# A four-layer block on one core: another order of the instruction lists of three engines in layer 1

## The reference, cut to what matters

```python
xn = _layernorm(x)                      # x already holds layer 0, its experts' output included
# attention: 16 heads of 64, causal
q, k, v = (einsum('bsd,hda->bhsa', xn, W) + b for W, b in ((Wq, bq), (Wk, bk), (Wv, bv)))
pattern = softmax(where(causal, q @ k.T * scale, -100000.0))
x_attn = einsum('bsha,had->bsd', pattern @ v, Wo) + bo
# feed-forward: both operands rounded to FP4 in blocks of 16 along the last axis
def fp4_quant_dequant(x):               # blocks of 16: scale = max|x| / 6
    idx = searchsorted([0.25, 0.75, 1.25, 1.75, 2.5, 3.5, 5.0], abs(x / scale))
    return GRID[idx] * sign(x) * scale
h = silu(fp4(xn) @ fp4(w_gate).T) * (fp4(xn) @ fp4(w_up).T)      # 352 wide
x = x + x_attn + fp4(h) @ fp4(w_down).T
```

## Time and profile before

| what | us |
|---|---|
| median of three executions | 3218.11 (3212.95 to 3218.94) |
| the profiled execution, whole | 3212.44 |
| its span from first to last instruction | 3211.1 |
| busy in the span: PE | 2501.2 |
| busy in the span: DVE | 2231.2 |
| busy in the span: ACT | 1427.3 |
| busy in the span: POOL | 835.2 |
| granted clock of TensorE, mean | 0.904 |

### The profile page before, as it was taken

The page is one execution under the profiler, slowest core; times in us unless marked ns, Lnnn a source line. Parts: engine busy times, 40 slices in busy tenths (PEclk is TensorE's granted clock), DMA queues, the critical chain, the costliest instruction groups (busy, mean ns, idle before and its releaser), DMA issues.

```text
span 3211.1 us, 47743 instructions
## 1 busy us (share of the span) xinstructions
PE 2501.2 (78%) x18201; PEld 1749.2 (54%) x18201; DVE 2231.2 (69%) x4587; ACT 1427.3 (44%) x3688; POOL 835.2 (26%) x453
## 2 busy tenths in 40 slices
PE   4788888888887767888888888867999975677776
PEld 2455555556555654555656556544666663454444
DVE  3488888888887544666576666644666626999997
ACT  0344534544445114565555656532433333444443
POOL 0033343333444301222222222210000002333332
PEclk9899999999999877999999999977999997888887
DMA  1010110110111440000000000000000003444342
GB/s 58 21 34 28 47 35 28 41 41 28 41 41 40 136 168 1 1 1 1 1 1 1 1 1 1 1 32 13 27 27 14 8 25 109 147 128 153 127 152 86
DMA packets 71348, 147.97 MB, mean 46 GB/s; under 512 B 6864, under 2 KB 37072, under 8 KB 70608
## 3 DMA queue, kind: packets, MB, share of 16 engines
q1 hardware_dynamic: 69072, 140.73, 13.3%
q0 software_dynamic: 2048, 4.20, 0.4%
HBM read 135.20 MB, written 9.18 MB: 45 GB/s over the span
## 4 chain that ended last, share of the span: by engine, by line
PE 29%; DVE 16%; issue 13%; ACT 9%; POOL 5%; DMA 2%; SPq 0%; DVEq 0%; POOLq 0%; ACTq 0%
POOL h L2054 4%; ACT pr L1764 3%; PE psum L578 2%; DVE mx L1282 2%; PE psum L325 2%; PE psum L470 2%; PE psum L504 2%; PE psum L515 2%; PE psum L582 2%; PE psum L347 2%; DVE mx L1326 1%; PE psum L774 1%; ACT pt L1808 1%; PE psum L587 1%; POOL got L2045 1%
## 5 line engine op out<-in xcount | busy, mean ns | idle before, releaser
L2020 POOL TENSOR_TENSOR h<-h,Crep 128x1024 f32<-128x1024 f32 x128 | 383.5, 3006 | 700.9 <-DVE h L1444 700.9
L2002 POOL TENSOR_TENSOR pr<-pr,rsum 128x512 f32<-128x512 f32 x192 | 228.0, 1191 | 741.5 <-DVE rsum L1294 741.5
L1326 DVE TENSOR_REDUCE mx<-psum 128x4 f32<-128x1024 f32 (+1 forms) x192 | 228.9, 1216 | 111.8 <-PE psum L587 111.7
L1444 DVE TENSOR_TENSOR_SCAN h<-dA,h 128x1024 f32<-128x1024 f32 x128 | 291.8, 2294 | 2.4 <-ACT dA L1905 1.8
L774 PE MATMUL psum<-h,pack_wf 128*128 128x256 f32 x1024 | 254.3, 405 | 5.4 <-POOL h L2020 5.4
L2054 POOL TENSOR_TENSOR h<-h,Crep 128x1024 f32<-128x1024 f32 x64 | 150.7, 2355 | 346.2 <-DVE h L1203 346.2
L1808 ACT ACTIVATE pt<-psum 128x1024 f32<-128x1024 f32 x192 | 187.5, 1022 | 95.4 <-PE psum L589 95.3
L774 PEld LDWEIGHTS psum<-h,pack_wf 128*128 128x128 f32 x1024 | 206.7, 206 | 42.0 <-POOL h L2020 6.4
L1764 ACT ACTIVATE pr<-psum,nb 128x256 f32<-128x256 f32 (+1 forms) x512 | 211.8, 441 | 31.0 <-DVE nb L1286 31.0
L1905 ACT ACTIVATE dA<-delta,A 128x255 f32<-128x255 f32 x512 | 210.2, 495 | 12.2 <-DVE h L1444 10.8
L1435 DVE TENSOR_TENSOR h<-dtu,psum 128x512 f32<-128x512 f32 x256 | 163.9, 676 | 68.7 <-PE psum L761 61.9
(11 more groups left out here) (342 smaller groups left out, 5632.8 us busy)
## 6 DMA issues: line engine op xcount, KB each, us to landing
Crep<-c_rows SPq DMA_DIRECT2D x64, 512.0 KB, 3.8
Brep<-bc_rows SPq DMA_DIRECT2D x64, 512.0 KB, 6.5
Crep<-bc_rows SPq DMA_DIRECT2D x64, 512.0 KB, 5.7
w1r<-m_w SPq DMA_DIRECT2D x32, 256.0 KB, 5.6
w2r<-m_w SPq DMA_DIRECT2D x32, 256.0 KB, 5.4
pack_wf<-wf SPq DMA_DIRECT2D x1, 3192.0 KB, 13.4
slots<-zero SPq DMA_DIRECT2D x12, 256.0 KB, 3.0
w1s<-s_w SPq DMA_DIRECT2D x8, 256.0 KB, 2.8
```

The costliest lines, as they stand in the source:

```text
L1326: ve.e.tensor_reduce(mx[:, qb, 2 * h:2 * h + 2, groups[0]:groups[-1] + 1], k.psum[:, base:base + 2, :].rearrange("p i (n x) -> p i n x", n ...
L1444: ve.e.tensor_tensor_scan(flat(h), flat(k.dA[c][g % 2]), flat(h), 0.0, ALU.mult, ALU.add).then_inc(*k.set("scanned", 0, b, g, c))
L2002: po.e.tensor_tensor(p3, p3, bcast(k.rsum[n][:, 0:len(heads[r])], P * (q + 1), 2), ALU.mult).then_inc(*k.set("normed", 1, b, p, r))
L2020: po.e.tensor_tensor(h[:, :, :], h[:, :, :], k.Crep[n % 3][:, :, :], ALU.mult).then_inc(*k.set("hC", 0, b, g, c))
```

## The change

The due times are removed and a table takes their place. ORDER[layer][engine_generator] lists, for each generator, the positions of its pieces in that engine's list of a full step; merge takes the generator with the lowest next position. Where a step lacks a generator (the first and last steps) the positions of the others hold. No instruction is added or removed, no wait, no buffer and no size is changed; every semaphore wait stands in front of the same instruction as before.

The diff, cut to its core:

```diff
-def merge(*stages):
+def merge(order, *stages):
...
-            gen, first, last, steps = stage
-            live.append([first, n, gen, first, (last - first) / steps])
+    for n, (gen, name) in enumerate(x for x in stages if x is not None):
+        live.append([n, gen, iter(order[name])])
+    live = [[next(at), n, gen, at] for n, gen, at in live]
     while live:
-        now = min(live, key=lambda x: (x[0], x[1]))
-        slot = next(now[2], None)
-        if slot is None:
+        now = min(live, key=lambda x: x[:2])
+        if next(now[2], run) is run:
             live.remove(now)
         else:
-            now[0] = now[3] + slot * now[4]
+            now[0] = max(now[0], next(now[3]))
...
-STEP1, TURN1, PROJ1 = 8, 48, 8.8
-QKV1, V1 = tuple(2.2 + 4.2 * j for j in range(8)), (35, 38, 41, 44.5)
-GATE1, HQ1 = (14.3, 20.6), (42.2, 42.9, 43.9)
...
+ORDER = {
...
+    1: {
+        "pe_attend": (0, 4, 6, 7, 8, 11, 12, 13, 15, 19, 20, 21, 23, 24, 28, 29, 32, 33, 34, 35, 36, 39, 40, 41, 43, 44),
+        "pe_ffn": (1, 16, 17, 22, 45, 46, 48, 50),
+        "pe_pre1": (2, 5, 9, 10, 14, 18, 25, 26, 30, 31, 38, 42, 47, 49),
+        "pe_spread1": (3, 27, 37),
+        "ve_attend": (0, 3, 4, 5, 16, 17, 18, 19, 20, 21, 23, 25, 26, 28, 32, 33, 34, 38, 41, 42, 44, 46, 49, 51, 56, 57, 60),
+        "ve_ffn": (6, 7, 8, 9, 10, 11, 12, 13, 14, 15, 22, 24, 27, 29, 30, 31, 36, 37, 39, 40, 43, 47, 50, 61),
+        "ve_pre1": (1, 48, 52, 55, 58),
+        "ve_spread1": (2, 35, 45, 53, 54, 59),
...
@@ (every generator, here pe_spread1)
-    yield 26
+    yield
     pe.wait_ge(*(k.at("hh", b - 2, 1) if b >= 2 else k.at("x_spread", 0) if b else k.at("wT", 8)))
     pe.e.transpose(bk[0:E0, 256:256 + D], k.oall[:, b, :], w["ident"]).then_inc(*k.set("o_turned", b))
-    yield 28.5
+    yield
...
-def steps1(k, b, attend, ffn, pre, spread):
+def steps1(k, b, e, attend, ffn, pre, spread):
...
-    T = TURN1
-    merge((attend(k, b), 0, T, T), (ffn(k, b), 0, T, T) if b < NB else None,
-          (pre(k, b + 1), 0, T, T) if b + 1 < NB else None,
-          (spread(k, b + 2), 0, T, T) if b + 2 < NB else None)
+    merge(ORDER[1],
+          (attend(k, b), e + "_attend"), (ffn(k, b), e + "_ffn") if b < NB else None,
+          (pre(k, b + 1), e + "_pre1") if b + 1 < NB else None,
+          (spread(k, b + 2), e + "_spread1") if b + 2 < NB else None)
```

## The result

The changed kernel takes 3093.92 us (median; 3093.20 to 3096.56) against 3218.11 us: 0.9615 of the time before, with an interval of 0.9599 to 0.9631. The profiled execution takes 3093.92 us, its span is 3092.6 us, against 3212.44 and 3211.1.

A forecast was written before the change was run, and what follows sets the result against it. DVE's late-starting list behind hh q1 was taken to set layer 1's tail, with PE waiting. A 50.1 us step saves 6.4 us for 15 steps, 96, plus 2 in the last: 98 off 3218.11 gives 3120 us, range 3096 to 3184.

The forecast's parts named there:

- the end of the step as placed: Layer 1, hand-placed lists: the step ends at 49.3 us, against 55.66 in the step placed from.
- the 0.8 us added to it: Layer 1 step: 49.3 us raised to 50.1, because the step placed from was short, 55.66 against a mean of 56.52.
- the last full step: End of layer 1: hh q1 earlier, only down, values and projection following; gain 0 to 4 us, taken as 2.
- The placing: Layer 1: each piece set at the later of its engine's last end and its operands' ends, giving predicted starts.
- So PE's clock is not what sets the tail.: Layer 1 tail: no clock fall before V1 one step later, yet 2.57 us wait and a 57.25 us step.
- the core of the change: Layer 1, xqT and gates before their neighbours: hh q1 ends at 24.9 instead of 29.0, 4.1 us earlier.
- nothing is gained there: Layer 1 tail from scores P0': 10.35 us against 10.39.
- free the scores of p5: Layer 1, q and k parts in pairs: no score waits behind them; scores p5 start at 33.7 instead of 36.8.
- The reading that DVE's list sets the tail: Layer 1: DVE's list after hh q1 takes 27 us, starts late, and sets the tail.
- Traded waits: Rival, layer 1: ACT's or DVE's list slips where cover is thin; step of 54 us, 3180 us; chance 0.22.
- The clock: Rival, PE in layer 1: more half clock from the new tail's gaps makes it slower, up to 3257 us; chance 0.08.
- A hidden ring: Rival, layer 1: a missed ring, such as block b+2's normalisation, holds the step; within 0.2%, 3218 us; chance 0.05.

The follow-up runs named there:

- The clock kept up: Kernel before plus six idle matmuls ahead of PE's wait for oe and six ahead of its wait for V0; 3221.29 us, ratio 1.0001.
- the second execution of before: The kernel before, unchanged, profiled once more; 3218.66 us, ratio 1.0000, span 3211.1.
- single parts: Changed kernel with the q and k parts put back singly on PE, and QK6 and QK7 behind exp p4r1 on ACT; 3084.84 us, 0.958.
- the kernel with three parts: Kernel before with gates early, the tail's order and the experts' spread late; 3139.50 us, ratio 0.9745.

## Why the forecast was right in its placing and wrong in its sum

Three terms of the sum failed: the end of the step as placed (49.3 us, measured 48.57), the 0.8 us added to it on the reading that the clock doesn't set the tail, and the last full step (2 us, measured 5.9 to 7.5).

**The placing.** Predicted and measured starts, T from the scores of p1: scores p2 7.1 and 7.21; p3 19.0 and 18.71; p4 26.5 and 26.44; p5 33.7 and 33.41; P0' 39.0 and 39.21; end of hh q1 24.9 and 24.66. The clock stays at 1.00. The waits for oe and V0 are gone. QK5 and QK7 wait 0.93 us each (0.9 and 0.8 predicted). Up to P0' nothing is off by more than 0.3 us.

**The end of the step** is at 48.57, where 49.3 was predicted. This is a term mis-sized: the tail from P0' takes 9.36 us, not 10.35. fp4 h ends at 42.8 instead of 43.4. DVE's records overlap by some 0.08 us where I had set them end to end; that this is the reason is likely, but no run shows it. V2 doesn't wait (1.1 us predicted), and V3 waits 0.26 us (0.6).

**The 0.8 us added to the step** failed as a step of reasoning, and so did the sentence of the prediction that it rests on: "So PE's clock is not what sets the tail." Before, steps of 55.66 and some 57 us take turns. I had looked at V1 in one of 57.25 us, found the clock at 1.00 there, and took the swing for something that any order of that kind has. The windows under "The clock kept up" show what it is: both kinds of step are at hq after 46.83 us, and the long one runs behind hq at a clock of 0.84. The wait of 1.97 us for hqT, which the earlier trace rows show without a fall behind it, had one in the next step. V3 took 1.60 us there instead of 1.02, values p4 1.98 instead of 1.09. The new tail has no such wait and its clock is 1.00, so its steps are all short ones, and the mean loses 0.9 us beyond what I placed. The tail's order alone already does this: its steps are 52.61 us, but for three of 53.3 with half clock at P0'. Three kernels on the way to the changed one swing again, by 1.6 to 3.2 us and mostly ahead of hq, where the clock falls around QK5 and the scores of p4 in their long steps; the copies early end that too.

**The last full step** falls by 7.5 us, where I took 2 of 0 to 4: 46.44 to 38.98. In the second execution of before it is 44.88, which makes it 5.9. I counted only hh q1 there. The granted clock over this step was 0.77 in the one shown and 0.81 in the second, and is 0.96 in the changed kernel. With the tail's order alone the step is 44.20 us (0.82), with the copies early 41.16 (0.89). How much of the 7.5 us is the clock and how much the order, no run separates.

**The sum.** In the two profiled spans, 118.5 us were gained. By marks: the first projection 6.3 us earlier, 14 steps 112.9 us, the last step 7.5 us, and behind it 8.2 us lost (1071.3 us before, 1079.5 after). Against the second execution of before: 4.8, 110.7, 5.9, and 2.9 lost, 118.5 again. In my sum of 98 us, one step of 6.4 stands for the first, 14 of 6.4 are 89.6, and 2 for the last. The miss is the step, 21 to 23 us (some 0.7 us of it the mis-sized end and 0.8 the swing), and the last step, 4 to 5.5 us, less the 3 to 8 us behind layer 1. Between the medians the miss is 26 us, since the profiled execution of before was 5.7 us below its median and that of the changed kernel is its median.

**The loss behind layer 1**, 8.2 us, is for 5.4 us not the change's: the second execution of before, with no edit at all, is longer there by as much. The turn of 25.6 us in layer 2 is in one profiled execution alone; that second one and every other kernel here have 26.3 or 26.4 us. The 2.9 us that are left stay open. All kernels laid out by the new code have 1078.1 to 1082.8 us there, with the same instructions in the same order, and both executions of before have less. What makes an execution take the short turn is open too.

**The credit for the gain** was put in the wrong place, and this is the larger error, though the total hid it. The prediction calls the early gates "the core of the change", says of the tail "nothing is gained there", and of the pairs that they free the scores of p5. Adding the parts one by one to the kernel before gives, in us per step, in the mean and for the short steps (the shortest length that recurs among the first 13):

| added | mean step | gain | short step | gain |
|---|---|---|---|---|
| before | 56.52 | | 55.66 | |
| tail's order | 52.71 | 3.8 | 52.61 | 3.1 |
| gates, xqT, hh early | 51.51 | 1.2 | 50.17 | 2.4 |
| spread late | 51.20 | 0.3 | 49.80 | 0.4 |
| ACT's copies of q, k early | 48.52 | 2.7 | 48.53 | 1.3 |
| DVE's list and the turn of o | 47.69 | 0.8 | 47.76 | 0.8 |
| pairs on PE (the changed kernel) | 48.46 | -0.8 | 48.57 | -0.8 |

The row of DVE's list is the difference of two kernels. The short steps are those in which no half clock counts: from "gates" on they have none at all, and those of before and of the tail's order are as long with falls ahead of hq as without (55.65 us where the idle matmuls took the falls away). Between them the gains hardly depend on the order of adding: gates alone 2.5 us, the spread alone 0.3, DVE's list ahead of the copies 0.8. The exception is the spread undone at the end, 0.85. The means do depend on it (gates alone 1.7, DVE's list ahead of the copies 1.3), by what each kernel loses to the clock: 0.9 us before, 0.1 with the new tail, 1.3 with the gates early, 1.4 with the spread late, nothing from the copies on. So the early gates are worth twice what their row of the mean shows, and the copies half; the tail's order is first in either column. The tail's place rests on more than that order: from hq to the next scores it is 5.75 or 5.76 us in every kernel with the new tail (5.88 in the one with less work on DVE; 6.5 in a few steps of two kernels with half clock there), whether hq is ready at 46.86, 44.04 or 42.81. In the kernel before it is 8.83 at full clock. The early gates are real too: 2.4 of the 4.1 us by which the prediction had hh q1 earlier reach the step.

Why I missed it: I compared the tail from P0' on, 10.39 us against 10.35. But P0' itself had been moved, from behind V1 to ahead of it, and values p4 from behind hq to ahead of it. A length measured from a mark that the change moves says nothing of what the change does there. From the end of hq, which no edit of the tail moves, it would have been 5.9 us in my own placing (43.4 to 49.3) against 8.8 in the earlier trace rows.

**The reading that DVE's list sets the tail** is half right for the kernel before and wrong for the changed one. DVE was busy for 19.08 of 19.48 us, yet starting that stretch 4.5 us earlier moved its end by 2.5 us in a step at full clock; 1.49 us of the rest are a wait for the scores of p4. In the changed kernel 1.8 us less work moved it by 0.4. Busy isn't bound.

**The rivals.** Traded waits: there are some, 0.93 (three times), 0.69 and 0.63 us, and single parts win back 0.8 us of them. The placing held 5.6 us of idle time on PE, with QK5's and QK7's in it; the step has 4.7. The clock: seven gaps a step of up to 0.93 us, and 1.00 over 685 us. By the page of the Trainium skill that I named for this rival, "TensorE: Matmul & The Clock Gate", its section on depth-cycling, frequent short idles could have set the clock oscillating; the trace of this kernel doesn't show it. The clock did come and go in kernels on the way, behind a wait of 2.26 us. A hidden ring: none; the normalised block is in time.

## What to carry to other kernels

Measure a stage's tail from the end of the piece that arrives last, not from one that the change moves; then ask of each instruction behind that point whether it could stand ahead of it. Here that meant the scores, turns and values of attention ahead of the turns of hq, and it gave 3.8 of 8 us. A copy that another engine waits for belongs ahead of exponentials and takes that nobody waits for yet (2.7 us here, half of it through the clock), and two dependent parts back to back cost the wait between them (0.8 us). Where steps of one kernel swing, compare two of them, cut at the piece that arrives last and with the clock beside each part, before a mean is taken; here parts that seemed not to add in the mean add within 0.02 us in steps at full clock. When a hand placing agrees with the result, its total is tested, its attribution isn't: only kernels with single parts show that.

## What the runs showed of the hardware

What a fall of the clock costs depends on where it lands. Ahead of hq in the kernel before it costs nothing, since the next wait takes it up: 46.83 us at 0.93 and at 1.00, with one step in 13 that lost 0.6 us. Behind hq it costs 1.6 us: 10.42 us at 0.84 against 8.83. At the scores of p4, in the kernel with three parts, a step at 0.93 is 2.5 us longer than one at 1.00. One and the same wait, 1.97 us for hqT or 2.26 us for a copy of k, was followed by half clock in one step and by full clock in another.

A VectorE instruction beside GpSimd's division is slower in the changed kernel too. The clamp of q0, 0.34 us in the kernel before where no division ran beside it, now falls beside one. First DVE, then POOL:

```profile
1401.37 1.08 DVE L1625 TENSOR_SCALAR he<-he 128x352 f32<-128x352 f32 x1
```

```profile
1401.21 1.04 POOL L2051 TENSOR_TENSOR pr<-pr,rsum 128x512 f32<-128x512 f32 x1 [1.36 <-DVE rsum L1340]
```

The clamp takes 0.7 us longer, and ACT, which starts its next piece of q0 at 1402.48, right behind the clamp, and DVE's hh q0, which waits 0.76 us for ACT, come as much later. It ends there: the maxima of p3 follow at 1404.54, and their scores, with the mask, end at 1404.47 only. The Trainium skill, "SBUF — State Buffer", section "SBUF: two separate sides", describes the lock that would do this; the trace agrees, with 1.08 against 0.34 us.

The same instructions of layer 2 ran with a turn of 25.59 or 26.30 us in two executions of one kernel. Over 13 turns that is 9 us, of which 5.4 were left behind layer 1 as a whole. A profile of one execution carries differences of that size, and a sum set against its span should say so.
